# Output rows of a dense mixture stored by indirect scatters from GpSimd instead of block stores from SyncE

## What is computed

```python
def _L1_ffn_ref(x, gate_w, gate_b, w1, b1, w2, b2):
    logits = jnp.einsum('bsh,he->bse', x, gate_w) + gate_b
    topk_vals, topk_idx = jax.lax.top_k(logits, K)            # K = 2 of E = 8 experts
    topk_weights = jax.nn.softmax(topk_vals, axis=-1)
    mask = jax.nn.one_hot(topk_idx, E, dtype=topk_weights.dtype)
    weights = jnp.einsum('bske,bsk->bse', mask, topk_weights)
    h = jax.nn.relu(jnp.einsum('bsh,ehf->bsef', x, w1) + b1)   # all 8 experts, F = 256
    expert_out = jnp.einsum('bsef,efh->bseh', h, w2) + b2
    return jnp.einsum('bseh,bse->bsh', expert_out, weights)
...
    h = h + _L1_ffn_ref(_layernorm(h, axis=-1), ...)           # the output, 8320 x 128 float32
```

## Time and profile before

| what | us |
|---|---|
| median of 3 executions | 2296.66 (2294.49 to 2298.24) |
| the profiled execution, whole | 2295.27 |
| its span from the first instruction to the last | 2293.5 |
| the last stage in it, from POOL's first copy to the span's end | 1745.6 to 2293.5 |

### The profile page before, as it was taken

The page is one execution under the profiler, slowest core; times in us unless marked ns, Lnnn a source line. Parts: engine busy times, 40 slices in busy tenths (PEclk is TensorE's granted clock), DMA queues, the critical chain, the costliest instruction groups (busy, mean ns, idle before and its releaser), DMA issues. The chain is left out here.

```text
span 2293.5 us, 69970 instructions
## 1 busy us (share of the span) xinstructions
PE 2092.2 (91%) x27103; PEld 1589.8 (69%) x27103; DVE 1215.6 (53%) x3749; ACT 988.4 (43%) x2969; POOL 616.7 (27%) x853
## 2 busy tenths in 40 slices
PE   6999987999898997766997999999978999999999
PEld 2444445676676675465554788888846999999999
DVE  0000056777777775697226455555545555555555
ACT  0000024555555553212432555555524555565555
POOL 0000004777777775010000334343410000000000
PEclk9999978999999999756997999999978999999999
DMA  7776500000000000100000000000000000000000
GB/s 299 292 296 275 229 0 2 4 3 3 3 3 3 3 3 14 70 1 0 0 0 0 2 3 2 2 2 2 2 1 3 8 8 8 8 8 8 7 8 10
DMA packets 22322, 91.72 MB, mean 40 GB/s; under 512 B 5092, under 2 KB 13548, under 8 KB 15596
## 3 DMA queue, kind: packets, MB, share of 16 engines
q1 hardware_dynamic: 20302, 86.00, 9.6%
q10 hardware_dynamic: 1822, 2.68, 0.4%
HBM read 84.41 MB, written 4.26 MB: 39 GB/s over the span
## 5 line engine op out<-in xcount | busy, mean ns | idle before, releaser
L1395 ACT ACTIVATE hidden_m<-ps,s_f_b 128x128 f32<-128x128 f32 x1040 | 296.3, 368 | 224.9 <-PE ps L1338 221.4
L805 PE MATMUL ps<-xn,s_a_wqkv 128*128 128x260 f32 x1024 | 288.7, 406 | 12.7 <-ACT qk_a L551 8.0
L1338 PE MATMUL ps<-xn,s_f_w 128*128 (+1 forms) x2080 | 286.8, 282 | 1.1 <-ACT hidden_m L1395 1.1
L153 PE MATMUL ps<-x_chunk,s_w_tok 128*128 128x512 f32 x576 | 254.1, 600 | 21.5 <-DMA s_cls<-in_cls 21.5
L1474 DVE SCALAR_TENSOR_TENSOR acc_m<-ps,weights_m,acc_m 128x128 f32<-128x128 f32 x520 | 182.3, 351 | 154.1 <-ACT acc_m L1418 105.2
L1338 PEld LDWEIGHTS ps<-xn,s_f_w 128*128 128x128 f32 x2080 | 254.5, 193 | 9.0 <-ACT hidden_m L1395 1.3
L1350 PE MATMUL ps<-s_f_w,hidden_m 128*128 128x128 f32 x2080 | 253.6, 275 | 0.0
L1350 PEld LDWEIGHTS ps<-s_f_w,hidden_m 128*128 128x128 f32 x2080 | 242.6, 192 | 1.6
L153 PEld LDWEIGHTS ps<-x_chunk,s_w_tok 128*128 128x128 f32 x576 | 109.1, 192 | 164.5 <-issue 143.0
L805 PEld LDWEIGHTS ps<-xn,s_a_wqkv 128*128 128x128 f32 x1024 | 175.9, 192 | 56.9 <-ACT qk_a L551 20.5
L1324 POOL COPY xn_tile_m<-xn 128x128 f32 (+1 forms) x65 | 19.1, 293 | 561.4 <-PE ps L1377 494.2
(11 more groups left out here) (193 smaller groups left out, 4297.4 us busy)
## 6 DMA issues: line engine op xcount, KB each, us to landing
x_chunk<-in_x_main SPq DMA_DIRECT2D x48, 1536.0 KB, 9.4
out<-acc_m SPq DMA_DIRECT2D x65, 64.0 KB, 1.5
s_f_w<-in_f_w SPq DMA_DIRECT2D x2, 1024.0 KB
x_chunk<-in_x_tail SPq DMA_DIRECT2D x16, 96.0 KB, 12.4
s_w_tok<-in_w_tok ACTq DMA_DIRECT2D x1, 1216.0 KB, 9.5
s_a_wqkv<-in_a_wqkv ACTq DMA_DIRECT2D x1, 768.0 KB
s_a_wqkv<-in_a_wqkv SPq DMA_DIRECT2D x1, 768.0 KB
s_f_w<-in_f_w SPq DMA_DIRECT2D x2, 256.0 KB
```

The source lines that it names most:

```text
L153: nc.tensor.matmul(ps[:, a.slot, :], w_tok[:, k, :], xb[:, a.slot, k, :], start=(k == 0), stop=False)
L805: nc.tensor.matmul(ps[:, QK_BANK[i], 0:QUAD], w_qkv[:, c * P:(c + 1) * P], xn[:, t.h * QUAD:(t.h + 1) * QUAD], start=True, stop=True).then ...
L1338: last = nc.tensor.matmul(ps[:, b % 2, i * P:i * P + n], w1[:, c * P:(c + 1) * P], xn[:, bass.ds(a.index * n, n)], start=True, stop=True)
L1395: last = nc.scalar.activation(hid[:, a.slot, c, :], ps[:, b % 2, i * P:i * P + n], ACT.Relu, bias=b1[:, c:c + 1])
```

## The change

SP no longer has a program in this stage. POOL stores instead: it computes once the table of the row numbers of all tiles (`out_rows_m`, 128 x 65 int32, entry (p, t) is 128 t + p), and stores each tile by an indirect transfer, which takes the 128 row numbers from one column of that table. POOL's program, a loop before, is written out for all 65 tiles. In iteration i POOL copies tile i, then waits for the additions of tile i-2 and stores it; the final waits for the stores are POOL's too.

```diff
+        rows = sb("out_rows_m", [P, tokens // n], mybir.dt.int32)
+        rows_set = sem("out_rows_set_m")
...
-        @block.sync
-        def _(sp):
-            def step(j, at):
-                a = at(2)
-                if a:
-                    sp.wait_ge(acc_done, E1 * a.index + E1)
-                    sp.dma_start(out[bass.ds(a.index * n, n), :], acc[0:n, a.slot, :])\
-                        .then_inc(stored[a.slot], 16)
-            pipelined(sp, tokens // n, SL, D_, SL, step)
-            for i in range(SL):
-                sp.wait_ge(stored[i], 16 * len(range(i, tokens // n, SL)))
-
         @block.gpsimd
         def _(pool):
-            def step(j, at):
-                a = at(0)
-                if a:
-                    since(pool, l_ps, a.index, SL)
-                    since(pool, base_ps, a.index, SL)
-                    cols = bass.ds(a.index * n, n)
-                    nc.gpsimd.tensor_copy(xs[:, a.slot, :], xn[:, cols])
-                    nc.gpsimd.tensor_copy(hs[:, a.slot, :], h[:, cols]).then_inc(copied, 1)
-            pipelined(pool, tokens // n, SL, D_, SL, step)
+            tiles = tokens // n
+            nc.gpsimd.iota(rows[:, :], [[n, tiles]], base=0, channel_multiplier=1).then_inc(rows_set, 1)
+            pool.wait_ge(rows_set, 1)
+            for i in range(tiles + D_):
+                if i < tiles:
+                    if i >= SL:
+                        pool.wait_ge(l_ps, i - SL + 1)
+                        pool.wait_ge(base_ps, i - SL + 1)
+                    cols = slice(i * n, (i + 1) * n)
+                    nc.gpsimd.tensor_copy(xs[:, i % SL, :], xn[:, cols])
+                    nc.gpsimd.tensor_copy(hs[:, i % SL, :], h[:, cols]).then_inc(copied, 1)
+                if i >= D_:
+                    o = i - D_
+                    pool.wait_ge(acc_done, E1 * o + E1)
+                    nc.gpsimd.indirect_dma_start(out[:, :], bass.IndirectOffsetOnAxis(ap=rows[0:n, o:o + 1], axis=0),
+                                                 acc[0:n, o % SL, :], None).then_inc(stored[o % SL], 16)
+            for i in range(SL):
+                pool.wait_ge(stored[i], 16 * len(range(i, tiles, SL)))
```

## The result

Over 17 executions of each kernel, the median is 2300.38 us after and 2294.69 before; the ratio is 1.0028, with a 95% interval from 1.0015 to 1.0041 (the two medians alone give 1.0025). The forecast was +2.0 us; what came is +5.7 by the medians, and +6.8 by the spans of the two profiled executions. The time lies inside the stated range, and just beyond the 0.2% that I had given 24%. I had also written that the forecast is wrong over 2301.3, which is 4.6 above the old median.

The account below looks back on a forecast made before the run. PE alone was taken to bound the steady part, leaving only the stage's ends to change. Steady part 0, start +0.5 and end +1.5 gave +2.0 us on the median 2296.66, so 2298.7 us; range 2294.8 to 2306.0.

Parts of the forecast that it names:

- Steady part, 0: The 62 tiles between the stage's ends: a scatter of about 1.0 us on POOL makes PE wait nowhere, cost 0.
- the cover: Time per step that a scatter may hold POOL's queue before PE waits: 4.13 + 2.74 = 6.87 us.
- Start, +0.5: Stage's start: the iota and the wait for it stand ahead of POOL's first copy, on the path; +0.5 us, at most 1.1.
- End, +1.5: After the last additions: POOL writes out the transfers (+1.0 us) and they land in 2.0 instead of 1.5 (+0.5).
- My upper end for it, 6.9 us: Upper bound of the cost at the stage's end: the longest scatter that would still be hidden in each step, +6.9 us.
- First use at the start: Rival, stage's start: POOL's first iota pays a first-use cost, 1.8 to 7.5 us instead of 0.5; upper half 10%.
- VectorE kept out: Rival, each tile: POOL's scatter makes DVE stand; at 3.1 us a scatter 48 us more, about 2347; 5%.
- the first-byte times of the Trainium skill: Stage's end: about 1 us to a transfer's first byte from GpSimd, 0.6 from SyncE; end +0.4, sum 0.9.
- two rivals that cost each tile: Scatter holds POOL beyond 6.87 us (8.3 us each, about 2394; 6%), or POOL's scatter keeps VectorE out (about 2347; 5%).
- a long store: Part of the forecast's own 76%: a long first store puts the time over 0.2% slower; 3%.

## Where the prediction was right, and the step that failed

- **Steady part, 0: right.** The scatter's hold on POOL, 1.0 us as I took it from a POOL product of like length, is 0.97. Steps are 8.31 us, and the cover that I read out of the earlier trace rows is borne out within 0.4 us by the runs with five scatters, which cost nothing, and six, which do.
- **Start, +0.5: right in kind, half as large.** +0.25 us. The IOTA row is 0.18 us, below the copy's 0.29 by which I had bounded it, and the wait behind it costs less than the 0.17 that I had added.
- **End, +1.5: the term that failed.** Its two parts were fair: wake-up, writing out and landing came to +0.95 (0.28 us to wake and 2.24 until the landing is seen, against 0.03 and 1.55 on SP), where I had +1.5 from 1.0 for the writing out and 0.5 for the landing. What is missing is a third part, the DRAIN, +5.37. I took "the program waits for the last store" to be the end of POOL's program, and asked only how long the store takes. The end of a stage is a flush of each engine and a barrier, and the change made POOL's flush the last of all. The profile before has no row for it in the groups, since it is not counted as busy; it stands on L1262, with 0.56 us at 2273.6. Even with that row the 5.37 could not have been read, because POOL issued no transfer there. The whole term is +6.3 where I had +1.5. My upper end for it, 6.9 us, took that in, but it stood for a scatter that holds POOL that long, and none does. That the measured time lies in my range is luck.
- **First use at the start: did not happen.** The first iota has no gap before its row but the barrier, and the first scatter of all holds POOL 1.18 us instead of 0.97 and lands after 3.9 instead of 2.2, inside the cover. By the 6 us that the Trainium skill gives for a first call ("GPSIMD Engine Reference", section "2.1 Instruction dispatch"), the start would have cost over 20 times the 0.25 us; no such call shows here.
- **VectorE kept out: in the last part of a scatter only, and it costs nothing.** One instruction is touched, a cast that falls beside the scatter. Its group in the stretch from 1762 to 2285 before, and then after, with the group whose wait gives the time back:

```profile
L1449 DVE CAST index_m<-index_m 128x2 f32<-128x2 uint32 x63 | 10.6, 169 | 2.2
```

```profile
L1448 DVE CAST index_m<-index_m 128x2 f32<-128x2 uint32 x63 | 16.0, 254 | 2.2
...
L1450 DVE TENSOR_SCALAR weight_sum_m<-exp_gap_m 128x1 f32<-128x1 f32 x63 | 9.7, 154 | 53.8 <-ACT exp_gap_m L1403 53.8
```

  The mean of 254 ns mixes two kinds. In the step shown above the cast begins 0.59 us after the scatter, takes 0.35 us and ends at 1913.88, just before the scatter does (1913.91). In the next step it begins 0.37 us after the scatter, well inside its 0.97 us, and takes the old 0.17:

```profile
1921.34 0.97 POOL L1322 DMA_INDIRECT out<-acc_m,out_rows_m  x1 [4.13 <-DVE acc_m L1473]
1921.71 0.17 DVE L1448 CAST index_m<-index_m 128x2 f32<-128x2 uint32 x1
```

  So it is for all 63: the 30 casts that begin 0.59 to 0.64 us into the scatter end 0.03 us before it, and the 33 that begin at 0.47 or earlier are not held. Where POOL issues no transfer (the run with the iota and the written-out program alone), all take 169 ns. Of the rule on the shared ports that the prediction cited from "SBUF — State Buffer", section "🔬 SBUF: two separate sides", of the Trainium skill, the trace agrees that one engine can hold the other up; that it does so for a whole instruction is not what it shows, since the early casts run through. The 5 us in total come out of VectorE's wait for the exponential, 53.8 us now and 59.3 before.
- **By the first-byte times of the Trainium skill** ("DMA: Bandwidth & Descriptors", section "Latency and other measured facts"), the end would have cost +0.4. The trace has +0.95 for wake-up and landing, without the DRAIN.
- **The chances.** Over 0.2% slower had 24%, and 21 of them were for two rivals that cost each tile and one at the start. What decided was at neither place. The other 3 were for the right place, the end, but for a long store. As a forecast of size, 2.0 us where 5.7 to 6.6 came is too small by a factor of three.

## What to carry to other kernels

Before work is moved to another engine at the end of a stage, list what that engine still does after its last instruction there, the closing flush included, and ask which engine's flush is last afterwards. If GpSimd issues transfers, keep the end free of them, or flush GpSimd earlier where it is idle: in this kernel two stores left with SyncE, or one line, took 6.3 and 5.2 us of the tail back. And when an experiment adds load to one engine, see that it leaves the programs of the others as they are; two runs here measured something else.

## What the hardware showed that I had not expected

- A DRAIN on GpSimd takes 0.054 us plus 0.0818 per transfer that GpSimd has issued since the last DRAIN (1, 32, 63 and 65 transfers of 64 KB; 0.136, 2.672, 5.208 and 5.372 us), and 65 plain ones cost the same 5.37 as 65 indirect ones. It clears the earlier transfers while the last is still under way, but does not end before that has landed (2291.0 after a landing at 2290.9). Beyond 65 the line breaks off.
- An indirect store of 128 rows of 512 bytes holds GpSimd's queue 0.97 us, and in a row they come 1.26 us apart; a plain store of the same bytes holds it 0.54 us. They land 2.2 and 1.8 us after the issue, SyncE's in 1.5.
- An indirect store holds up a VectorE instruction only in its last part: casts of 0.17 us that began up to 0.47 us into the store's 0.97 were as quick as ever, and those that began at 0.59 or later ended with it, after 0.31 to 0.35 us.
- Three more semaphore waits in ScalarE's loop came with a stand of 2.4 us in each pass of the loop, with nothing left to wait for; its cause is open.
